# Attention, one ring of seven PSUM banks, an MLP moved behind the last unit, and row transfers flushed only when needed

## The reference

```python
# block 0, c = the first two rows of ctx_1024, halves x0, x1 of 1024 rows
mod = silu(c) @ ada_w + ada_b                       # 9 shifts, scales and gates
x0 += g_msa * mha(mod(ln(x0)));  x1 += g_msa * mha(mod(ln(x1)))      # within a half
ox = attend(q(xm), k(ym), v(ym)) @ crs_proj_w       # xm, ym = mod(ln(x0)), mod(ln(x1)): each half
oy = attend(q(ym), k(xm), v(xm)) @ crs_proj_w       # looks at the other half
x += g_mca * (ox, oy);  x += g_mlp * mlp_gelu(mod(ln(x)))
# block 1
x = ln(x + mha(x, x, x, mask))                      # only keys among the last 512 pass the mask
x = ln(x + mha(x, ctx, ctx))                        # ctx has 1601 rows
x = ln(x + relu(x @ w1 + b1) @ w2 + b2)
```

## Time and profile before

| | us or share |
|---|---|
| median of 3 timed runs | 2152.79 |
| profiled execution | 2160.66 |
| its span, first to last instruction | 2158.8 |
| PE busy | 1969.9 (91%) |
| DVE busy | 1559.6 (72%) |
| ACT busy | 1293.2 (60%) |
| POOL busy | 540.9 (25%) |
| mean granted TensorE clock | 0.957 |

### The profile page before, as it was taken

How to read it: one execution, slowest core, us unless ns; L and a number is a source line. 1 busy time by engine, 2 the same in 40 slices (tenths; PEclk the granted TensorE clock), 3 DMA queues, 4 the chain that set the end, 5 groups by cost and what they waited for, 6 DMA issues and landing times. The chain is left out here.

```text
span 2158.8 us, 33694 instructions
## 1 busy us (share of the span) xinstructions
PE 1969.9 (91%) x12890; PEld 767.6 (36%) x12890; DVE 1559.6 (72%) x2905; ACT 1293.2 (60%) x2406; POOL 540.9 (25%) x409
## 2 busy tenths in 40 slices
PE   5899799898989999999988998899999999999976
PEld 3333233232323343433524433222335235335325
DVE  4767788787967858568365567888994995996804
ACT  1146576565756676757766655457874874784660
POOL 1135784572032311022111334302010101101100
PEclk9689999999999999999999999889999999999998
DMA  6724423432044302033043444220020020000000
GB/s 152 146 82 112 127 69 85 106 80 50 17 117 73 80 21 56 16 66 72 3 106 60 98 108 100 63 46 19 7 48 3 17 44 3 14 17 4 14 17 12
DMA packets 96249, 125.61 MB, mean 58 GB/s; under 512 B 25261, under 2 KB 80926, under 8 KB 90958
## 3 DMA queue, kind: packets, MB, share of 16 engines
q1 hardware_dynamic: 93774, 122.84, 24.2%
q10 hardware_dynamic: 2304, 0.53, 0.1%
HBM read 88.90 MB, written 24.74 MB: 53 GB/s over the span
## 5 line engine op out<-in xcount | busy, mean ns | idle before, releaser
L1703 ACT ACTIVATE PT<-ps 128x512 f32<-128x512 f32 (+1 forms) x2112 | 1109.6, 601 | 649.8 <-PE ps L1488 631.6
L1786 DVE TENSOR_REDUCE mx<-ps 128x1 f32<-128x512 f32 x2048 | 1281.9, 681 | 206.4 <-PE ps L1509 203.6
L1488 PE MATMUL ps<-QS,KS 51*128 51x512 bf16 (+3 forms) x4224 | 809.0, 385 | 15.9 <-DMA QS<-mr 15.5
L1509 PE MATMUL ps<-KS,QS 49*128 49x512 bf16 x2048 | 730.6, 392 | 94.5 <-DVE mx L1786 52.7
L1535 PE MATMUL ps<-PT,Vt 128*32 128x512 f32 (+1 forms) x4224 | 575.4, 617 | 0.0
L1509 PEld LDWEIGHTS ps<-KS,QS 49*128 49x128 bf16 x2048 | 188.4, 94 | 679.1 <-DVE mx L1786 433.6
L1488 PEld LDWEIGHTS ps<-QS,KS 51*128 51x128 bf16 (+3 forms) x4224 | 236.7, 96 | 235.5 <-ACT PT L1703 57.8
L2057 POOL TENSOR_TENSOR OD<-ON,OD 128x1024 f32<-128x1024 f32 x15 | 35.4, 2359 | 488.8 <-DMA OD<-scr_r 488.8
L1535 PEld LDWEIGHTS ps<-PT,Vt 128*32 128x32 f32 (+1 forms) x4224 | 83.8, 108 | 143.6 <-issue 141.3
L1630 PE MATMUL ps<-XT,big 128*128 128x256 f32 x512 | 123.9, 392 | 4.2 <-ACT big L1759 3.6
L1642 PE MATMUL ps<-big 128*128 128x256 f32 x512 | 114.6, 382 | 1.6 <-DVE big L1930 1.6
(11 more groups left out here) (110 smaller groups left out, 1112.6 us busy)
## 6 DMA issues: line engine op xcount, KB each, us to landing
scr<-S SPq DMA_DIRECT2D x27, 768.0 KB, 3.8
big<-in_mask_1x1xSxS_ik SPq DMA_DIRECT2D x16, 1024.0 KB, 5.8
QS<-scr SPq DMA_DIRECT2D x32, 384.0 KB, 9.3
KS<-scr SPq DMA_DIRECT2D x24, 384.0 KB, 8.7
QS<-scr SPq DMA_DIRECT2D x32, 256.0 KB, 6.1
ON<-Oe SPq DMA_DIRECT2D x256, 32.0 KB, 2.0
OD<-scr_r SPq DMA_DIRECT2D x32, 256.0 KB
KS<-scr SPq DMA_DIRECT2D x24, 256.0 KB, 4.9
```

The source lines that it names most:

```text
L1488: z = eng.matmul(ps[0:w, it.bank[1 - j], :], KS[lo:hi, part, pr, col:col + w], QS[lo:hi, part, u.qs, pr, :], start=part == 0, stop=part == ...
L1509: return eng.matmul(mbank(it)[:, 0:w], QS[lo:lo + MR, 0, u.qs, pr, 128 * it.tq:128 * it.tq + 128], KS[lo:lo + MR, 0, pr, it.lo:it.hi], sta ...
L1703: eng.activation(PT[0:w, it.pt * 4 + 2 * it.pp + 1 - k, :], ps[0:w, it.bank[k], :], ACT.Exp, scale=0.25).then_inc(S["exp_done"], 1)
L1786: eng.tensor_reduce(out=mx[:, u.b, c, it.i:it.i + 1], in_=mbank(it)[:, 0:it.hi - it.lo], axis=AX.X, op=ALU.max).then_inc(S["max_done"], 1)
```

## The change

There are three edits, and nothing that is computed changes.

1. `take_bank` hands out banks 0 to 6 in one ring, to `s` and to all users of `take_m` alike, in the order of the plan. `s` waits for whatever empties its two banks; each exponential frees one bank.
2. The MLP of chunk 0 (last but one in the order) is held until the last unit begins (`ended.add("last")`). There `mlp1_first` brings `xt` and the first half (4 `hid`, one `mout`). Its second half is in `between`, which stands ahead of `last_l1`, with the first two steps of the last chunk's normalisation (`norms[:2]`: reciprocal and the DMAs through DRAM) issued before it. Its layer norm and store come in `last_l1` after the fourth `hid`.
3. When a chunk's first maxima begin, `flush_later` and `flush_slow` run only if the query slot isn't filled or one of the unit's key rows is still due (`due_keys`). `l0_weights("crs")` is held back 6 steps in `slow`, the chains for keys and values begin with `flush_slow`, and the waits in `ln_mod` for the crossing attention (`g` = 1) are shorter by one step at three pieces.

```diff
--- before.py
+++ after.py
@@ -187,11 +187,14 @@
             n[name] += by
             return n[name]
 
+        def take_bank():
+            b = n["bank_use"] % 7
+            n["bank_use"] += 1
+            return b, mark.get(("m_bank", b), [])
+
         def take_m(it):
 
-            it.mb = 4 + n["m_use"] % 3
-            n["m_use"] += 1
-            it.m_need = mark.get(("m_bank", it.mb), [])
+            it.mb, it.m_need = take_bank()
             it.m_ready = up("m_ready")
 
         def give_m(it, *values):
@@ -284,6 +287,8 @@
                 it.hi, it.rest, it.mid, it.low = up("hi_done"), up("rest_done"), up("mid_done"), up("lo_done")
                 mark[("qf_free", quick) if quick else "xn_free"] = ("lo_done", it.low)
                 ends.append(lambda: split_end(it))
+                if not q:
+                    due_keys.add(("k", name))
                 if quick:
                     flush_ends()
                     quick_rows.append((lambda: to_dram(it), lambda part: to_rows(it, (part,))))
@@ -321,6 +326,7 @@
                     mark["scr_free", it.k] = (it.lo_sem, up(it.lo_sem, 32))
                     if not q:
                         mark["klo", name] = mark["scr_free", it.k]
+                        due_keys.discard(("k", name))
                 if 0 in parts:
                     dma(it, name, 4)
                     if q:
@@ -450,9 +456,7 @@
                 it.u, it.i, it.pp = u, i, pp
                 it.q_in, it.m_in, it.mask = n[f"q_in{u.qs}"], mark["m", u.hg, u.qs], n["mk_step"]
                 it.q_lo = n[f"q_lo{u.qs}"]
-                it.bank = [(n["a_use"] + k) % 4 for k in range(2)]
-                it.a_need = [max(0, n["a_use"] + k - 3) for k in range(2)]
-                n["a_use"] += 2
+                it.bank, it.a_need = zip(*[take_bank() for k in range(2)])
                 up("s_ready", 2)
                 it.s = [n["s_ready"] - 1, n["s_ready"]]
                 if pp == 0:
@@ -460,7 +464,8 @@
                     n["key_tiles"] += 1
                 it.pt = u.slot[i]
                 it.pt_free = mark.get(("pt_free", it.pt), [])
-                up("exp_done", 2)
+                for k in range(2):
+                    mark["m_bank", it.bank[k]] = [("exp_done", up("exp_done"))]
                 xs[i, pp] = n["exp_done"]
                 if i == len(kts) - 1 and pp == 1:
                     mark["qs_free", u.qs] = ("s_ready", n["s_ready"])
@@ -714,6 +719,7 @@
         taken, held_rows = [False, False], {}
         quick_rows = []
         slow = []
+        due_keys = set()
 
         def flush_slow():
             while slow:
@@ -819,13 +825,16 @@
             for i, (ph, c, qs, hg) in enumerate(seq):
                 u = Unit(ph, c, qs, hg)
                 fg = exp_steps(u, held)
+                if i == len(seq) - 1:
+                    ended.add("last")
                 for f, after in fg[:-1]:
                     if not left and k + 1 < total and (k == 0 or step >= opens[k]):
                         k += 1
                         if every[k][3] == 0:
                             bg_until(unit0[0] + k)
-                            flush_later()
-                            flush_slow()
+                            if not taken[every[k][2]] or any(key in due_keys for key in every[k][0].kdep(every[k][1])):
+                                flush_later()
+                                flush_slow()
                             assert taken[every[k][2]]
                         left = start(k)
                         m = len(left)
@@ -874,12 +883,12 @@
             held()
 
         def ln_mod(c, g):
-            return (stats_steps(c, 1e-6, 0, 4) + xnorm_steps(c, 7 if g == 0 else 3)
-                    + [(3, lambda: do_xt("mod", c, g))])
+            return (stats_steps(c, 1e-6, 0, 4 if g != 1 else 3) + xnorm_steps(c, 7 if g == 0 else 3 if g == 2 else 2)
+                    + [(3 if g != 1 else 2, lambda: do_xt("mod", c, g))])
 
         def kv_l0(c, g, slot=None):
             over = mark.get("ks_over", []) + mark.get(("half_over", c // 2), [])
-            return (ln_mod(c, g) + (q_steps(c, slot, 4 * g) if slot is not None else [])
+            return ([(0, flush_slow)] + ln_mod(c, g) + (q_steps(c, slot, 4 * g) if slot is not None else [])
                     + k_steps(512 * c, 512, f"k_in{c}", over, 4 * g) + v_steps(4 * c, 512, c, over))
 
         def q_l0(c, slot, g):
@@ -947,7 +956,20 @@
             return ([(4, lambda: do_xt("x", c))] + mlp_chain(c, True, 24, None, (0, 0)) + ln_l1(c, 2, 0)
                     + [(0, lambda: store(c))])
 
-        def last_l1(c):
+        def mlp1_first(c):
+            return [(4, lambda: do_xt("x", c))] + [(hp % 2, lambda hp=hp: do_hid(c, True, 24, 0, hp)) for hp in range(4)] + [
+                (2, lambda: do_mout(c, 0, 2, None, (0, 0)))]
+
+        def between(c):
+            flush_outs()
+            for f in norms[:2]:
+                f[1]()
+            del norms[:2]
+            for hp in range(4):
+                do_hid(c, True, 24, 1, hp)
+            do_mout(c, 2, 2, None, (0, 0))
+
+        def last_l1(c, other=()):
 
             at["tail"] = True
             flush_norms()
@@ -961,6 +983,8 @@
             do_lnscale(c, 1, 1, 2, 2)
             for hp in range(1, 4):
                 do_hid(c, True, 24, 0, hp)
+            for f in other:
+                f()
             do_xt("x", c, cols=256, t0=2)
             do_mout(c, 0, 2, None, (0, 0))
             do_hid(c, True, 24, 1, 0)
@@ -1084,7 +1108,7 @@
         work.post(8, kv_l0(2, 0))
         work.post(8, kv_l0(3, 0))
         work.post(8, q_l0(2, 0, 0), 2)
-        work.post(8, q_l0(3, 1, 0) + [(0, lambda: l0_weights("crs"))], 3)
+        work.post(8, q_l0(3, 1, 0) + [(0, lambda: slow.append([6, lambda: l0_weights("crs")]))], 3)
         side.extend([lambda kind=kind, g=g: modulation(kind, g) for g in (1, 2) for kind in ("mod_t", "mod_g")])
         side.append(lambda: gate_bias(0, I["L0_xattn_attn_proj_b"]))
         side.extend([lambda t=t, k=k: scan(t, k) for t in range(NT) for k in range(4)])
@@ -1178,9 +1202,13 @@
             def post_ca(c, qs):
                 if c == 1:
                     norm(c % 2, True)
-                    work.post(99, [(0, lambda: need_o("ca")), (None, lambda: last_l1(c))], 2)
+                    work.post(99, [(0, lambda: need_o("ca")), (0, lambda: between(0)),
+                                   (None, lambda: last_l1(c, [f for _, f in ln_l1(0, 2, 0)] + [lambda: store(0)]))], 2)
                     return
                 end_l1(99, c, "ca")
+                if c == 0:
+                    work.post(99, [("ca0", lambda: None), ("last", lambda: None)] + mlp1_first(c))
+                    return
                 work.post(99, [(f"ca{c}", lambda: None)] + mlp1(c))
 
             p1, p3 = phase_l0(1, post), phase_ca(512, 4, post_ca)
@@ -1484,7 +1512,8 @@
                 col, vt, w = u.kts[it.i]
                 pr, lo, hi = 2 * u.hg + it.pp, 64 * j, 64 * j + KROWS[part]
                 if part == 0:
-                    q.wait_ge(S["exp_done"], it.a_need[1 - j])
+                    for name, v in it.a_need[1 - j]:
+                        q.wait_ge(S[name], v)
                 z = eng.matmul(ps[0:w, it.bank[1 - j], :], KS[lo:hi, part, pr, col:col + w], QS[lo:hi, part, u.qs, pr, :],
                                start=part == 0, stop=part == 1 and not u.ph.masked, tile_position=(lo, 0))
                 if part == 1 and u.ph.masked:
```

## The result

The median of five runs is 2131.28 us (2127.64 to 2138.29) against 2152.83 for the kernel before (2144.44 to 2155.91). The ratio is 0.9902, with a 95% interval of 0.9883 to 0.9921: 21.5 us faster, where I had forecast 35. The two profiled executions lie 33.0 us apart (2160.66 and 2127.64), because the one of before is above all its timed runs and the one of after is the fastest of its own.

A forecast was written before the change was run, and what follows sets the result against it. DVE's score reductions bound pure attention, PE the stretches with an MLP; -16.8 (held MLP), -11.5 (ring) and -6.7 (transfers) sum to -35.0 us: 2125.7 from the profiled 2160.66, 2118 as timed median, range 2086 to 2152.

The forecast's parts named there:

- The held MLP: Chunk 0's MLP moved into and behind the last unit: -16.8 us in sum, between -25 and -5.
- Together 34.6 us leave the stretch before the last unit: Before the last unit: 31.0 us freed by moving chunk 0's MLP, plus 3.6 us of its DVE work.
- 13 x 1.97 = 25.6, plus xt ...: 42.9: Last unit with the MLP's first half: PE bound, 42.9 us instead of 28.3, a cost of 14.6 us.
- the end: After the last pv: the MLP's second half makes out start 5.6 us later, with 3.5 back and 1.1 more.
- the higher clock: At the end, PE not coming from idle: out gains 1.5 us and the next hid 2.0, together 3.5 us.
- The ring: Seven PSUM banks shared by scores and maxima: -11.5 us, from 7.5 for activation waits and 4 for the burst around 1410.
- I take the 7.5: PE's idle time ahead of maxima for the MLP's activations, where DVE idles too, counted as 7.5 us gained.
- rival (c): After DVE's statistics and normalisations: late reductions hold back scores too, up to 67 us over 111 waits, 2196; chance 0.07.
- Rival (d): Cycling the ring's banks makes PE's clock swing: one key tile in ten at 1.2 GHz, +74 us, about 2203; chance 0.02.
- Transfers by need: Row transfers, weight loads and background chains: -6.7 us, from 2.7 for later weights and 4 for shorter waits.
- Holding the weights back should give the difference, 2.7 us: PE's wait for QS<-mr near 268 us: 2.7 us less, at best 7.6 and some slow clock, at worst nothing.
- The three shorter waits: Background chains: up to 21 steps, some 26 us, freed; taken as -4 us, with bounds of -20 and +10.

The follow-up runs named there:

- end_only: Kernel before with the held MLP alone, of which only the second half moved behind the last unit: 2140.75 us, ratio 0.9947.
- hybrid_tail: hybrid with the moved second mout of chunk 0 split in two, one half before out and one after it: 2109.65 us, ratio 0.9773.
- all_parts: hybrid_tail plus the third edit (transfers by need, later weights, shorter waits): 2111.41 us, ratio 0.9791.
- hybrid: Kernel before with seven-bank ring and moved second MLP half, but old four and three banks while a first-layer MLP runs: 2117.28 us, ratio 0.9814.
- flush_only: Kernel before with the third edit alone (flush on need, later weights, shorter waits): 2157.86 us, ratio 1.0024.
- ring_first: Kernel before with the seven-bank ring for the first unit's maxima alone, four and three banks from unit 1 on: 2156.75 us, ratio 0.9991.

## Why the prediction was right and wrong

**What bounds.** Right: the pure stretches keep 2.48 us for a key tile, and DVE sets it. The profiled pair even gives my sum, -33.0 for -35.0, but by its spread. By the medians three terms have to be mended.

**The held MLP**, -16.8 forecast, -11 measured (-7 to -16 by the interval). Two steps failed first, both by a line that I read too quickly. "Together 34.6 us leave the stretch before the last unit": unit 61 lost 17.6 (67.2 in before to 49.6 in end_only). "13 x 1.97 = 25.6, plus xt ...: 42.9": the last unit got no MLP and shows 25.3 with the ring, 27.5 without. I took the mark `"last"` for what it is called, and didn't look who else adds it. The two errors nearly cancel. When the hold is real, its sizes are right: the last unit takes 42.2 us for 42.9, and unit 61 loses another 16.6 for 17.0 (34.6 - 17.6). Then the term that was mis-sized is the end. `out` starts 17.4 us after the last `pv` instead of 11.3, +6.1 for +5.6, with the gap of 2.11 us that I expected. What I counted against it, -3.5 for the higher clock, didn't come in full. In the kernel after `out` is 2.8 us shorter (3.72), of which I had counted half, but `hid` only 0.5 of the 2.0 (8.58, where I had 7.07); in end_only they take 5.41 and 10.07, against 6.52 and 9.05. The pause of 4.45 us ahead of `xt`, which I had left as it was, is what the clock falls in, as hybrid_tail shows. The 1.1 us by which DVE's 7.5 should stick out of `mout`'s 7.17 were a slip: the difference is 0.3. PE's waits behind the second `xt` grow by about 0.4 in the kernel after. From the last `Oe` to the end of the span the kernels with the moved half (hybrid_tail and all_parts apart) need 71.7 to 74.8 us, and those without 67.1 to 67.8: +4 to +7 instead of +3.2. In end_only's trace -17.6 in unit 61 and +7.1 at the end make -10.5, which is the measured -11.

**The ring**, -11.5 forecast, -13 measured (-8 to -18). The size is right and the places are wrong. "I take the 7.5", PE's waits of maxima for the MLP's activations, failed. These waits moved onto the scores (8.5 us of L1517 in the waits of after, and 7.1 of `mout` for PT), and there they cost 12 to 15 us, as hybrid shows. That is rival (c)'s mechanism, with a gelu in place of a reduction, beside four MLPs instead of at 111 places. By these numbers the ring without it would be worth some 25 us instead of 13, an estimate. The gains that I hadn't in the sum are the first unit, about 9 us, by an earlier rise of the clock, and units 17 and 18, some 2 to 6: where the third part is out they take 71.5 to 72.6 us together with the old banks and 66.1 to 69.6 with the ring, for a reason that I haven't traced. The burst near 1410 gave about 2 (unit 46: 40.1 to 38.1) for 4, and the last unit 2.2, from 2.175 to 1.97 us a key tile, which I had counted under the hold. Rival (d), the rule of the Trainium skill, TensorE: Matmul & The Clock Gate, A second HAM failure mode (psum-queue depth-cycling), isn't borne out where I placed it: with seven banks in turn pure attention has 1.00. Beside the gelus, where the ring does make PE idle briefly, the clock fell to 0.94, as the rule would have it, because a producer held a bank and not because the banks turn.

**Transfers by need**, -6.7 forecast, +5 measured alone (+1.5 to +9), 0 to +5 in company. "Holding the weights back should give the difference, 2.7 us" was right as to the direction, and the wait is gone altogether, not only the 2.7. (The 7.57 was one execution's figure: kernels with the weights in their old place show 2.2 to 4.9 us there.) It failed as a term of the time, since the early gain is given back in later units, and the new wait near 440 us is one of the signs that I had named for being wrong. The flush on need also does what it says: the result of unit 33 is copied out at 1140.75 and its DMA leaves at 1141.36, where it took 12 us. It may have paid more than the 1 us that I allowed: units 33 to 35 together take 74.7 to 75.5 us in the five traces with the flush on need and 76.7 to 79.7 in the nine without. Which wait that saves I haven't traced. "The three shorter waits ... -4, with bounds of +10 (they clump elsewhere)": the bound was the truth about the mechanism, and the value that I took had no row behind it.

So of the 13.5 us between forecast and result, the third part holds about 12 (from -6.7 to +5) and the end about 5; the ring's 2 and what the three parts give more together than alone go the other way. What is not settled: which transfer or flush makes units 17, 20, 26 and 28 longer with the later weights, and how much of flush_only's 5 us is the clock's own spread.

## What to carry to other kernels

Before pooling buffers, ask for each producer how long it holds one: a pool ties every user to the slowest holder, and the one that feeds the longest chain should keep buffers of its own beside it. A step that is moved pays only if the engine that is late in the new place differs from the one in the old; when both are bound by PE, the move is worth nothing, however idle the others look. When a change depends on a mark or a key, follow every place that sets it before costing what it gates.

## What the runs showed of the chip

The clock multiplies short waits, and it makes equal programs differ. Unit 46 has the same instructions and nearly the same waits in end_only and in ring_first, and takes 40.1 us in the one and 42.8 in the other, with the granted clock at 0.80 and 0.66. First end_only, then ring_first:

```profile
1371.20:1411.30 40.10, 32.46 (x142) 9.13 (x141) 30.58 (x54) 10.54 (x19) 10.16 (x6) 0.80 0.07 24
```

```profile
1376.60:1419.40 42.80, 36.67 (x142) 10.44 (x141) 30.72 (x54) 10.49 (x19) 10.17 (x6) 0.66 0.07 22
```

PE has the same 142 matmuls in both and needs 32.46 us for them in one and 36.67 in the other, though it stands idle 1.5 us less in the slower one. What set the two clocks apart no row shows. In the two places where I read a price from the traces, a stall weighed a multiple of itself: some 2 us of waits near 100 us made about 9, and 1.5 us in unit 26 with 1.3 just ahead of it made 5.7. I had priced each wait at its own length.
